# The last batch's attention moved to another chain of an eight-stage kernel, with other buffers and a new order

## The reference, cut to what matters

```python
# s0 (state space), then s1 (8 experts and a shared one, top 2)
x = x + tanh(g_xattn[0]) * ssm(ctx, layernorm(x), ...)         # 16 states, a scan over 256 steps
x = x + tanh(g_ffn[0]) * experts(layernorm(x), Wr, Wg, Wu, Wd, Wsg, Wsu, Wsd)
# s2 (int8 products with smoothing), then s3 (ternary weights)
x = x + tanh(g_xattn[1]) * quant_expert(layernorm(x), fside, ctx)
x = x + tanh(g_ffn[1]) * swiglu_ternary(layernorm(x), W_up, W_gate, W_down)
# s4 (queries and their norms) and sa (the attention proper), then s5 (int8 activations)
def L2_xattn(hidden, ctx, Wq, Wk, Wv, Wo, gq, gk):             # 16 heads of 128
    q, k, v = rmsnorm(hidden @ Wq, gq), rmsnorm(ctx @ Wk, gk), ctx @ Wv
    attn = softmax(einsum('bqhd,bkhd->bhqk', q, k) / sqrt(128))
    return einsum('bhqk,bkhd->bqhd', attn, v).reshape(B, S, H * D) @ Wo
x = x + tanh(g_xattn[2]) * L2_xattn(layernorm(x), ctx, ...)
x = x + tanh(g_ffn[2]) * bit_mlp(layernorm(x), w_gate, w_up, w_down, ln_weight)
# s6 (one small attention), then s7 (ternary weights, root mean square)
x = x + tanh(g_xattn[3]) * cross(layernorm(x), ctx, Wq, bq, Wk, bk)
x = x + tanh(g_ffn[3]) * swiglu_ternary7(layernorm(x), w_gate_up, w_proj)
```

## Time and profile before

| what | value |
|---|---|
| median of 3 runs | 1062.55 us (1059.73 to 1063.28) |
| the profiled execution's own time | 1062.66 us |
| its span, first to last instruction | 1060.9 us |
| TensorE busy | 860.6 us, 81% |
| VectorE busy | 713.6 us, 67% |
| ScalarE busy | 557.3 us, 53% |
| GpSimd busy | 276.0 us, 26% |
| mean granted clock of TensorE | 0.925 |

### The profile page before, as it was taken

One profiled execution on the slowest core, in us unless ns is written; L12 is line 12 of the kernel. 1 busy time (PEld: TensorE's weight loads), 2 busy tenths in 40 slices (PEclk: granted clock), 3 DMA queues, 4 the chain that ended last, 5 costly groups with the idle time before them and its releaser, 6 DMA issues.

```text
span 1060.9 us, 13344 instructions
## 1 busy us (share of the span) xinstructions
PE 860.6 (81%) x4116; PEld 616.7 (58%) x4120; DVE 713.6 (67%) x1716; ACT 557.3 (53%) x1318; POOL 276.0 (26%) x365
## 2 busy tenths in 40 slices
PE   3779988755898987798979789979998779699355
PEld 1435655534566865655757567558776656476134
DVE  3896789774548768976889866765568772244643
ACT  8887874222464654446535555653466534466313
POOL 1100212102244201630763113415310423200205
PEclk9999999977999999889999999989999979699568
DMA  7676455445422231341442035404411244111002
GB/s 263 190 249 213 150 170 161 136 161 167 142 90 75 90 105 60 90 125 45 123 151 85 11 114 166 135 25 134 135 61 58 60 126 119 45 31 30 30 1 70
DMA packets 56614, 116.53 MB, mean 110 GB/s; under 512 B 6232, under 2 KB 18400, under 8 KB 55392
## 3 DMA queue, kind: packets, MB, share of 16 engines
q1 hardware_dynamic: 47328, 90.51, 26.8%
q0 software_dynamic: 9216, 25.17, 8.2%
HBM read 97.74 MB, written 17.92 MB: 109 GB/s over the span
## 4 chain that ended last, share of the span: by engine, by line
PE 45%; DVE 22%; issue 16%; POOL 9%; ACT 7%; DMA 1%; POOLq 0%; DVEq 0%; SPq 0%; ACTq 0%
PE bk L1323 29%; PE bk L1402 7%; DVE ssm_u L1948 3%; PE bk L1611 2%; PE bk L1639 2%; DVE ssm_u L1942 2%; POOL aclB L922 1%; PE bk L1387 1%; POOL aclA L922 1%; POOL arA L902 1%; PE bk L1395 1%; DVE mx L2166 1%; POOL arB L928 1%; DVE lnbuf L1853 1%; POOL ring L993 1%
## 5 line engine op out<-in xcount | busy, mean ns | idle before, releaser
L1323 PE MATMUL bk<-hTA,ringT 128*128 128x256 f32 x448 | 109.2, 388 | 1.5 <-DMA ringT<-in_w 1.5
L856 POOL TENSOR_TENSOR lnbuf<-lnbuf,mhalf 128x2 f32<-128x2 f32 x32 | 23.3, 727 | 324.5 <-DVE lnbuf L1859 324.5
L1323 PEld LDWEIGHTS bk<-hTA,ringT 128*128 128x128 f32 x448 | 85.9, 195 | 16.6 <-issue 2.6
L1948 DVE TENSOR_TENSOR_SCAN ssm_u<-ssm_da,ssm_u 128x512 f32<-128x512 f32 x64 | 86.5, 1352 | 4.8 <-ACT ssm_da L1127 1.4
L1323 PE MATMUL bk<-qk 128*128 128x256 f32 x288 | 83.2, 416 | 4.5 <-ACT arB L1209 2.4
L1209 ACT ACTIVATE arB<-bk,nb,rqs 128x256 f32<-128x256 f32 x128 | 70.9, 560 | 24.0 <-DVE nb L2169 23.3
L1323 PE MATMUL bk<-arB,cx 128*128 128x256 f32 x256 | 72.3, 406 | 5.6 <-DVE qk L2205 3.5
L1127 ACT ACTIVATE ssm_da<-sdl,nega 128x255 f32<-128x255 f32 x128 | 57.1, 499 | 35.1 <-DVE ssm_u L1948 34.3
L902 POOL TENSOR_TENSOR arA<-t2A,arA 128x256 f32<-128x256 f32 x44 | 37.1, 844 | 131.6 <-DVE t2A L1981 130.1
L2166 DVE TENSOR_REDUCE mx<-bk 128x2 f32<-128x512 f32 x68 | 46.8, 688 | 32.2 <-PE bk L1323 32.0
L1323 PEld LDWEIGHTS bk<-qk 128*128 128x128 f32 x288 | 56.4, 207 | 19.8 <-issue 8.4
(11 more groups left out here) (339 smaller groups left out, 2172.5 us busy)
## 6 DMA issues: line engine op xcount, KB each, us to landing
ringT<-in_w SPq DMA_DIRECT2D x56, 384.0 KB, 3.4
...
```

The costliest lines, as they stand in the source:

```text
L1323: return t_.matmul(dst, lhsT, rhs, start=start, stop=stop)
L1948: v.tensor_tensor_scan(row, ssm_da[:, n % 2, :, :].rearrange("p e t -> p (e t)"), row, 0.0, ALU.mult, ALU.add).then_inc(*sig(K, "scan", n))
```

## The change

The last batch's attention (`LATE = B - 1`) leaves `rest(3)` and becomes the end of `middle(3)`, behind s4. There it uses the middle's and the front's banks and a part of `arA`, the region of the experts' stage, which batch 3 no longer needs by then. Its wait for the end of batch 2 falls away in favour of one for the last use of `Z0`; that wait moves to s5 of batch 3, which still uses the rest's banks. Its instructions are the same in number, shape and order. Every engine's whole `PLAN` is replaced by another one; of its 250 lines the diff below shows five pairs for TensorE.

```diff
+        LATE = B - 1
+        pmL, e0 = cut(arA, 0, 3, 2, S)
+        pTL, e0 = cut(arA, e0, 2, 2, S)
+        oTL, e0 = cut(arA, e0, 2, S)
+        HEAD = [(W0, W1, Z0, AT, pmL, pTL, oTL) if b == LATE else (SC, PT, OP, AR, pm4, pT4, oT4) for b in range(B)]
...
             "pe": {
@@ kq, batch 3 @@
-                    3: ((0, 3725.25), ... (10, 3751.47), (11, 3752.48), (11.52, 3753.69), ... (15, 3760.29), (15.52, 3763.27), (16.52, 3763.58), (16.9, 3765.27),)},
+                    3: ((0, 2762.65), ... (10, 2789.57), (13.52, 2795.85), (14, 2797.86), (14.52, 2797.87), (16.52, 2797.88), (16.9, 2812.83),)},
@@ s7, batch 2 @@
-                    2: ((3, 3746.69), (5, 3749.90), ... (13.4, 3756.06), (14.4, 3757.23), (16.2, 3758.24), ... (22.8, 3764.94), (24.6, 3764.95), (25.6, 3786.79), (30, 3813.00),),
+                    2: ((3, 2787.29), (5, 2789.30), (7.8, 2791.73), ... (11.6, 2798.80), (13.4, 2800.11), ... (16.2, 2805.80), (17.2, 2813.24), ... (25.6, 2817.51), (28.4, 2833.31), (30, 2844.47),),
@@ head, batch 3 @@
-                    3: ((-0.25, 3689.67), (1, 3844.38), (1.39, 3845.29), (2.64, 3888.40), ... (17.42, 4065.33),)},
+                    3: ((-0.25, 2807.27), (0.39, 2807.38), (1, 2813.64), (2.42, 2819.91), (2.64, 2829.12), (3.64, 2862.99), (4, 2864.90), ... (17.42, 2895.85),)},
@@ s2, batch 0 @@
-                "s2": {0: ((2, 1676.16), (5, 1688.61), (7, 1803.83), (10, 1882.42), (11, 1951.74), (15, 1991.92), ... (26, 2110.31),),
+                "s2": {0: ((2, 1524.66), (5, 1572.64), (7, 1579.28), (10, 1580.29), (11, 1585.60), (15, 1592.21), ... (26, 1694.64),),
@@ vo (value_output) @@
-                "vo": {0: ((0, 1633.09), (1, 1645.97), (2, 1657.50), (3, 1660.57), (4, 1670.52), (5, 1683.34), (6, 1836.67), (7, 1857.38),)},
+                "vo": {0: ((0, 1462.89), (1, 1479.70), (2, 1575.81), (3, 1575.82), (4, 1588.58), (5, 1588.59), (6, 1603.15), (7, 1609.26),)},
...
             def attention(b):
+                SCb, PTb, OPb_, ARb, pmb, pTb, oTb = HEAD[b]
                 yield at_head(b, -0.25)
                 pe.wait_ge(*at(b, "s4.dve", "rqs"))
-                if b:
+                if b == LATE:
+                    pe.wait_ge(*at(b, "r1.act", "wT"))
+                elif b:
                     pe.wait_ge(*at(b - 1, "s7.dve", "x", 1))
...
             def s5(b):
                 OPb = OP[:, :].bitcast(BF16)
                 yield at5(b, AT5["qT"])
+                if b == LATE:
+                    pe.wait_ge(*at(b - 1, "s7.dve", "x", 1))
                 pe.wait_ge(*at(b, "s5.dve", "hq"))
...
@@ middle and rest, the same on ScalarE, TensorE and VectorE @@
                 if b in EARLY4:
                     yield from s4(b)
+                if b == LATE:
+                    yield from attention(b)
 
             def rest(b):
                 if b not in EARLY4:
                     yield from s4(b)
-                yield from attention(b)
+                if b != LATE:
+                    yield from attention(b)
```

More of the change, by code:

```diff
@@ L350, in build @@
             "pe": {
[L351 to L356, removed]
[40 rows of a table removed]
@@ new lines, in build @@
+                "h1": {0: ((2.5, 525.14), (4.5, 526.28), (11.5, 535.36),),
+                    1: ((2.5, 1699.27), (11.5, 1700.88),),
+                    2: ((2.5, 2194.31), (11.5, 2199.47),),
+                    3: ((2.5, 2506.69), (11.5, 2515.64),)},
+                "head": {0: ((-0.25, 1918.16), (0, 1919.27), (0.39, 1919.28), (1, 1925.41), (1.39, 1926.67), (1.64, 1931.60), (2.39, 1931.61), (2.42, 1934.60), (2.64, 1936.74), (3, 1942.03), (3.25, 1944.22), (3.39, 1947.20), (3.42, 1947.31), (3.64, 1952.78), (4.25, 1952.79), (4.42, 1956.25), (4.64, 1957.34), (5.39, 1959.71), (6.64, 1964.35), (7.42, 1972.36), (7.64, 1974.07), (8.42, 1977.08), (8.64, 1996.37), (9, 1996.38), (9.42, 1999.22), (9.64, 2004.37), (10.39, 2004.38), (10.64, 2008.11), (11, 2008.12), (11.42, 2008.13), (11.64, 2010.81), (12, 2010.82), (12.25, 2010.83), (12.42, 2012.49), (12.64, 2014.35), (14, 2020.10), (14.25, 2021.31), (14.42, 2022.32), (14.64, 2022.33), (15.64, 2028.03), (16.25, 2029.21), (17.42, 2033.58),),
[40 rows of a table added]
@@ new lines, in build @@
+                "state": {0: ((-1.2, 121.14), (-0.2, 160.85), (0.8, 389.64), (1.8, 390.05), (3.95, 395.22), (4.95, 395.33), (5.8, 395.54), (6.95, 398.55), (7.8, 406.95), (8.95, 412.58), (9.8, 460.19), (9.95, 460.20), (10.8, 494.13), (13.8, 499.24), (14.95, 499.25), (15.95, 505.71), (16, 515.56),),
[3 rows of a table added]
+                "ternary": {0: ((0.4, -11.84), (1.4, 38.34), (2.4, 138.23), (3.4, 392.92), (4.4, 395.29), (5.4, 420.90),)},
+                "vo": {0: ((0, 1462.89), (1, 1479.70), (2, 1575.81), (3, 1575.82), (4, 1588.58), (5, 1588.59), (6, 1603.15), (7, 1609.26),)},
@@ new lines, in build @@
+                "head": {0: ((-0.14, 1918.01), (0.25, 1921.37), (0.81, 1923.12), (1.25, 1927.02), (1.81, 1928.79), (2.25, 1929.80), (2.44, 1932.90), (2.81, 1934.06), (3.44, 1949.32), (3.81, 1949.33), (4.44, 1955.34), (4.81, 1955.95), (5.44, 1959.63), (6.81, 1965.01), (7.25, 1971.85), (7.81, 1971.86), (8.25, 1990.16), (8.81, 1997.96), (9.25, 1997.97), (9.81, 2001.48), (11.25, 2005.98), (11.81, 2012.57), (12.25, 2012.58), (12.44, 2013.55), (12.81, 2016.86), (13.44, 2016.87), (13.81, 2018.10), (14.81, 2022.63), (15.25, 2027.51), (15.81, 2031.52), (18, 2034.36),),
[40 rows of a table added]
@@ new lines, in build @@
+                "state": {0: ((0, 338.10), (0.2, 379.90), (5, 394.54), (5.2, 399.05), (7, 415.06), (7.2, 415.07), (9, 415.08), (9.2, 426.26), (10.2, 433.97), (10.7, 470.81), (11, 470.82), (11.2, 494.92), (15, 506.16), (15.7, 510.67), (16, 510.68), (17, 514.63),),
[3 rows of a table added]
+                "ternary": {0: ((0.5, 103.15), (0.6, 103.16), (1.5, 131.67), (1.6, 147.40), (2.5, 147.41), (2.6, 371.39), (3.5, 391.58), (3.6, 399.03), (4.5, 399.04), (4.6, 417.16), (5.5, 419.93), (5.6, 456.50), (6, 493.30),)},
+                "w2": {0: ((0, 241.53), (1, 564.34),),
+                    1: ((0, 1717.53), (1, 1757.54),),
+                    2: ((0, 2025.82), (1, 2025.83),),
+                    3: ((0, 2449.87), (1, 2459.88),)},
@@ new lines, in build @@
+                "h1": {0: ((3, 519.61), (7.5, 519.72), (11.5, 537.18),),
+                    1: ((3, 1764.19), (7.5, 1840.50), (11.5, 1840.51),),
+                    2: ((3, 2192.59), (7.5, 2194.66), (11.5, 2206.86),),
+                    3: ((3, 2508.57), (7.5, 2511.66), (11.5, 2518.92),)},
+                "head": {0: ((0.35, 1918.23), (0.82, 1925.54), (1.3, 1925.55), (1.35, 1925.56), (1.72, 1930.62), (2.3, 1931.93), (2.72, 1938.18), (2.82, 1940.07), (3.3, 1943.19), (3.35, 1947.77), (3.72, 1984.13), (4.3, 1984.14), (4.35, 1984.15), (4.72, 1986.16), (5.3, 1986.17), (5.35, 1986.48), (6.3, 1986.49), (6.35, 1986.50), (6.72, 1986.51), (7.3, 1990.32), (7.72, 1991.82), (8.3, 1991.83), (8.35, 1991.84), (8.82, 1998.09), (9.72, 2001.85), (10.3, 2003.89), (10.35, 2004.30), (10.72, 2012.01), (11.3, 2012.02), (11.72, 2012.33), (11.82, 2012.34), (12.3, 2012.35), (12.72, 2018.59), (13.3, 2018.60), (13.72, 2018.91), (13.82, 2019.04), (14.3, 2019.15), (14.35, 2020.25), (15.3, 2024.94), (15.35, 2025.25), (15.82, 2027.44), (16.3, 2028.75), (16.72, 2042.11),),
[40 rows of a table added]
@@ new lines, in build @@
+                "state": {0: ((-1, 365.96), (4, 385.00), (6, 400.06), (7, 400.07), (8, 406.00), (9, 406.90), (10, 429.80), (11, 442.01), (12, 491.36), (14, 494.27),),
[3 rows of a table added]
+                "ternary": {0: ((0, -8.83), (0.5, 16.69), (1, 16.80), (1.5, 38.26), (2, 108.04), (2.5, 304.96), (3, 369.64), (3.5, 390.92), (4, 394.23), (4.5, 399.76), (5, 406.31), (5.5, 418.50),)},
+                "vo": {0: ((0, 1464.13), (1, 1567.90), (2, 1567.91), (3, 1585.92), (4, 1585.93), (5, 1593.94), (6, 1610.60), (7, 1621.61),)},
@@ L524, in build @@
+                "wb": {0: ((0, 540.15), (2, 544.69), (3, 545.50), (5, 555.90),),
+                    1: ((0, 1864.29), (1, 1864.40), (5, 1871.60),),
+                    2: ((0, 2212.81), (2, 2214.84), (3, 2216.99), (5, 2223.51),),
+                    3: ((0, 2528.66), (1, 2531.87), (2, 2531.98), (5, 2534.82),)},
             },
             "pool": {
[37 rows of a table removed]
-                "state": {2: ((0.95, 2741.65), (2.95, 2762.03), (5.95, 2779.17), (6.95, 2791.08), (9.95, 2848.39), (10.95, 2992.12), (12.95, 3006.79), (13.95, 3041.93), (14.95, 3117.24), (15.95, 3166.45),),
-                    3: ((0.95, 3210.22), (1.95, 3214.29), (2.95, 3220.77), (3.95, 3224.17), (4.95, 3230.79), (7.95, 3244.82), (8.95, 3245.83), (11.95, 3264.61), (12.95, 3375.56), (13.95, 3405.67), (15.95, 3407.68),)},
[37 rows of a table added]
@@ new lines, in build @@
+                "state": {2: ((0.95, 1903.23), (3.95, 1930.28), (4.95, 1932.05), (5.95, 1932.06), (6.95, 1938.33), (8.95, 1946.39), (9.95, 1978.20), (10.95, 2071.29), (11.95, 2071.30), (12.95, 2158.32), (13.95, 2184.65), (14.95, 2184.66), (15.95, 2190.37),),
```

(19 more changed lines are left out.)

58 lines of the change are left out of this document (20 added, 38 removed), and 386 rows, old and new, of the table PLAN.

## The result

After takes 1056.79 us in the median of 6 runs (1054.27 to 1059.02), before 1062.53 beside it; the ratio is 0.9948, with a 95% interval of 0.993 to 0.9966. The forecast was 1054, the range 1045 to 1066.

What follows compares the result with a forecast made beforehand. TensorE was taken as the limit in attention 3's steady part, a dependence chain after it; time could fall only where TensorE waits or is slow before 980.8. -6.8 - 2 = -8.8 against 1062.66 gave 1053.9, say 1054 us, range 1045 to 1066.

Steps and rivals of the forecast that it cites:

- the two terms, -6.8 and -2: Forecast changes in us: -6.8 around the last batch's attention, -2 from the new order in earlier stages.
- Step (1), the end of the queries: Batch 3's last queries beside s7(2): the last nq ends at 899.6 instead of 905.3, rqT comes at 903.3.
- Step (2), the mixed stretch: First four heads mixed with s7(2)'s rest: sc0 at 905.8, 16.7 us work plus 2.5 waits, sc4 at 925.0.
- Step (3), what is left: From sc4 to the attention's residual: 49.0 us as before, so attention ends at 974.0; the 80.0 us after stay.
- the local sum: Net forecast for the tail, from s7(2)'s start to the attention's end: -6.8 us.
- the locked chains: Rival, s7(2) and the heads: neither covers the other's waits, sc4 near 941, attention 9 us later, 1070 us; chance 0.15.
- Step (4), the order further up: Stages from 205 to 275 us: s2(0) could begin sooner, -2 us; plus or minus 5 for pieces in later stages.
- The sign named for it: At s3(0): a start 2 us earlier would bear out the -2 us expected from the order in earlier stages.
- my bounds of -8.3 to +5.2: Around s2(0): -8.3 us if held-back work is all hidden, +5.2 if both state steps delay the chain.
- The clock: Rival, sc0 to sc4: TensorE partly at 1.2 GHz again, costing 5 us more, up to 8; about 1060 us; chance 0.12.
- the bound of 6: Between the first two heads: the prediction is wrong if sc1 comes more than 6 us behind sc0.
- The order further up: Rival, around s2(0): state steps delay its small steps by 5.2 us, giving 1061, or 1064 with later losses; chance 0.13.

Runs made afterwards that it cites:

- e1: After's structure, but every engine in the order of before up to s3(3), then of after; against before 1051.02 us, ratio 0.9901.
- e10: After's structure, every engine in the order of before up to s3(0), then of after, a repeat measurement; 1042.69 us, ratio 0.9822 to before.
- e8: Before, with 72 useless matmuls set into TensorE's waits ahead of and within the last batch's attention; 1059.76 us, ratio 0.9959 to before.
- e4: After's code with the attention in the experts' buffers, but all engines in the order of before; 1063.04 us, ratio 1.0014 to before.

## Why the prediction was right, and where it wasn't

*The direction and the sum.* 1054 was forecast, 1056.8 measured, and -8.8 against a span shorter by 8.4. Between the medians it is only -5.7. And the two terms, -6.8 and -2, were -10.8 and +2.3; they erred in opposite ways. The second is itself the rest of a loss of 13.2 and a gain of 10.9 that the prediction had neither of. That the local mechanism was right is no luck, as e1 shows with 10.7 us between its medians; that the whole came so near to 1054 is.

*Step (1), the end of the queries: right.* `rqT` at 905.25 - 888.45 = +16.8, forecast +17. The two table loads stand back to back with their functions again, 901.62 to 905.10, so the row was the right price. The drain that the Trainium skill ("ScalarE: Activation LUTs", What ACT_TABLE_LOAD costs) puts beside a load shows in neither trace.

*Step (2), the mixed stretch: right in size.* `sc0` comes at +18.5, forecast +20 (2.5 us were put on the way from `rqT`; it takes 1.68). Then 19.3 us to `sc4` at +37.8, forecast +39. TensorE is idle for 1.4 of these 19.3 us, where 2.5 was put on waits, and the fall of the clock, on which nothing was put, took about as much again: in e1, whose clock stays at 1.00 from 904 to 920, `sc0` to `sc4` takes 17.9.

*Step (3), what is left: the step that failed.* "From `sc4` to the residual at 980.84 it is 49.0 us" took the row at 931.80 for `sc4`. It is `sc3`: the scores in the earlier trace rows start at 917.23, 921.61, 927.24, 931.80, which is four starts and three turns. One head of 3.41 was charged to the new order and not to the old. With 925.0 as `sc4`, `sc3` falls at 921.6, the residual at 970.6, and the local sum is -10.2; the measurement says -10.8. The mechanism was right, the term short by one head; the residual came at +83.9, forecast +88. The same misreading stands in the case of the locked chains, where `sc3` at 937 is 5 us and not 9 behind the old one. From `sc3` on it takes 49.9 us after and 49.0 before, and then 80.1 and 80.1: in this pair nothing else is hidden there.

*Step (4), the order further up: wrong.* I looked at 205 to 275, took -2, and gave the rest plus or minus 5 without a sign. The sign named for it, s3(0) 2 us earlier, came out as 13.2 later. The loss of 13.2 us at s3(0) is outside my bounds of -8.3 to +5.2, and most of it arises ahead of 205, in the 200 us that I hadn't read because no piece of the attention lies there: the first scan is 9.5 us later (46.78 against 37.27), h1(0) 8.9 (104.49 against 95.55), and by 200 us VectorE is 9.9 us of work behind. Only the 4.3 us between h1(0) and h1(1) would fit the bounds. e10 shows that it is carried to the end whole. The middle's gain of 10.9 was not foreseen either. It arises early, since from s4(0) to s2(1) after needs 87.6 us and before 106.3, and some of it is lost again later. Its cause was not taken apart, only that it doesn't depend on the late start.

*The rivals.* The clock did fall, to a mean of 0.61 over 908 to 912, some 3 us at half, not ten; beside e1, at full clock, it cost 1.4 us. The chains did not lock: `sc0` to `sc1` took 5.8 us, just below the bound of 6 that was named, but the heads behind it 5.3, 4.4 and 3.7, and `sc4` starts at 926.2. The order further up does take something back, 13 us in the front and not 5.2 in s2(0), and the middle, which no rival had, returns most of it. In the profile of e8 TensorE was busy for all of 914 to 922 at 0.50 and then had 0.93 in 922 to 926; before, with 1.9 us of work in 918 to 922, was still at 0.50 in 924 to 928. By that the rule of the Trainium skill ("TensorE: Matmul & The Clock Gate", What's actually happening), that activity releases the clock, agrees with the runs.

So a part of the tail's 10.8 us is clock and the rest is work side by side. The clock cost the heads of before 3.5 us from `sc0` to `sc3` beside e8's, and 2.0 beside e4's (928.01 - 915.42 = 12.6), and the fillers brought 4.4 by the medians. No run holds the clock of before and after alike, so the shares aren't exact.
